# Adding the causal part of the first query tile's scores on VectorE instead of TensorE

## The reference, cut to what matters

```
x = x + moe_0(x, cond)                       # shared expert, 8 routed experts, top 2
x = x + moe_1(x, cond)
x = x + hs,  h_new = tanh(h * leak + sigmoid(h @ Wh.T + z_t @ Wz.T + b) * z_t)   # 256 steps, one after another
q, k, v = split(x @ c_attn_w + c_attn_b)     # k and v get the image token in front
scores = where(kj <= qi + 1, q . k / sqrt(8), -1e4) + mask
x = x + (softmax(scores) @ v) @ c_proj_w + c_proj_b
```

## Time and profile before

| what | value |
|---|---|
| median of 3 runs | 479.17 us (478.98 to 481.24) |
| profiled execution, time | 479.9 us |
| profiled execution, span of the instructions | 478.1 us |
| TensorE busy | 442.8 us, 93% |
| VectorE busy | 309.3 us, 65% |
| ScalarE busy | 261.2 us, 55% |
| GpSimd busy | 85.9 us, 18% |
| last step of the recurrence ends | about 343.1 us |

### The profile page before, as it was taken

How to read it: one execution, slowest core, us unless ns; L and a number is a source line. 1 busy time by engine, 2 the same in 40 slices (tenths; PEclk the granted TensorE clock), 3 DMA queues, 4 the chain that set the end, 5 groups by cost and what they waited for, 6 DMA issues and landing times.

```text
span 478.1 us, 13039 instructions
## 1 busy us (share of the span) xinstructions
PE 442.8 (93%) x4530; PEld 310.0 (65%) x4530; DVE 309.3 (65%) x999; ACT 261.2 (55%) x885; POOL 85.9 (18%) x365
## 2 busy tenths in 40 slices
PE   3999999899999999999998998999998798999984
PEld 2787787667777777776756766566655464656652
DVE  6774666666656556656557665576449978569851
ACT  3552646545646556456474356654777159764461
POOL 7120313221413213213121121211100000000000
PEclk9999999999999999999999999999999999999995
DMA  8400000000000000000000000000000001001000
GB/s 314 149 12 8 6 0 1 3 0 1 3 0 2 2 2 1 1 2 1 1 1 4 1 1 2 1 3 2 2 4 22 2 2 23 6 3 26 2 4 22
DMA packets 11222, 7.70 MB, mean 16 GB/s; under 512 B 8983, under 2 KB 10263, under 8 KB 11159
## 3 DMA queue, kind: packets, MB, share of 16 engines
q1 hardware_dynamic: 10727, 6.61, 4.5%
q10 hardware_dynamic: 432, 0.27, 0.2%
HBM read 5.39 MB, written 1.05 MB: 13 GB/s over the span
## 4 chain that ended last, share of the span: by engine, by line
PE 70%; ACT 13%; DVE 11%; issue 4%; DMA 1%; POOL 0%; ACTq 0%; DVEq 0%
PE ybk L1035 17%; PE cbk L1200 11%; PE hid L1180 7%; PE ybk L1156 6%; DVE cbk L1529 4%; ACT dd L956 4%; ACT hb L882 3%; DVE wm L1443 3%; ACT hs L961 2%; PE hid L1132 2%; PE vbk L1180 2%; PE hid L1084 2%; PE hid L1060 2%; PE hid L1053 1%; PE hid L1021 1%
## 5 line engine op out<-in xcount | busy, mean ns | idle before, releaser
L1529 DVE TENSOR_TENSOR_SCAN cbk<-dd 128x24 f32<-128x24 f32 x256 | 55.7, 218 | 102.3 <-ACT dd L956 98.9
L1200 PEld LDWEIGHTS cbk<-hs,rec 128*128 128x128 f32 x512 | 76.4, 188 | 56.2 <-ACT hs L961 49.1
L1200 PE MATMUL cbk<-hs,rec 128*128 128x8 f32 x512 | 91.5, 251 | 7.7 <-ACT hs L961 3.7
L772 POOL TENSOR_TENSOR dd<-hs,leak 128x8 f32<-128x8 f32 x256 | 55.1, 215 | 233.0 <-ACT hs L961 230.4
L1035 PE MATMUL ybk<-hg,down 128*128 128x256 f32 x352 | 95.8, 398 | 0.5 <-DVE hg L1405 0.2
L961 ACT ACTIVATE hs<-cbk 128x8 f32<-128x8 f32 x256 | 45.3, 177 | 70.5 <-DVE cbk L1529 69.2
L956 ACT ACTIVATE dd<-cbk 128x8 f32<-128x8 f32 x256 | 46.4, 181 | 61.6 <-PE cbk L1200 60.1
L1180 PE MATMUL hid<-xsp,up 128*128 128x256 f16 x528 | 73.1, 277 | 2.4 <-ACT hb L882 0.6
L1035 PEld LDWEIGHTS ybk<-hg,down 128*128 128x128 f32 x352 | 60.7, 191 | 6.3 <-DVE hg L1405 0.9
L1180 PEld LDWEIGHTS hid<-xsp,up 128*128 128x128 f16 x528 | 49.7, 105 | 10.9 <-ACT hb L882 2.9
L1156 PE MATMUL ybk<-hb,vx 128*32 128x64 f32 (+1 forms) x1536 | 38.2, 223 | 2.5 <-ACT hb L947 1.9
(11 more groups left out here) (231 smaller groups left out, 661.0 us busy)
## 6 DMA issues: line engine op xcount, KB each, us to landing
qz<-up_in SPq DMA_DIRECT2D x3, 512.0 KB, 6.8
out_dram<-silu SPq DMA_DIRECT2D x4, 256.0 KB, 2.9
x<-x_in SPq DMA_DIRECT2D x7, 128.0 KB, 8.2
down<-down_in SPq DMA_DIRECT2D x1, 768.0 KB, 8.6
att<-att_in SPq DMA_DIRECT2D x1, 743.0 KB, 9.4
down<-down_in SPq DMA_DIRECT2D x1, 640.0 KB, 6.2
kp<-mrow SPq DMA_DIRECT2D x32, 4.0 KB
qz<-rows SPq DMA_DIRECT2D x32, 2.0 KB, 1.7
```

What stands on the lines that cost most here:

```text
L772: tts(dd[:, t % ZR, 1, :, 2], hs[:, t, :], leak[:, 0:1].broadcast_to([P, B]), ALU.mult).then_inc(decay, 1)
L1200: pe.matmul(cbk[c % 2][:, o:o + B], wh, hs[:, t, :], start=False, stop=True, skip_group_check=True).then_inc(gate_pre, 1)
L1529: nc.vector.tensor_tensor_scan(vps[chunk_of(t) % 2], dd[:, t % ZR, 0].rearrange("p b o -> p (b o)"), dd[:, t % ZR, 1].rearrange("p b o -> ...
```

## The change

The list of tiles whose causal part is added by TensorE becomes empty. So the 16 units of tile 0 lose their third matmul, 16 units SC come onto VectorE, the exponentials of tile 0 read `pt` after SC, and the banks of these units are freed by VectorE. As the planner gets other units and costs, it makes all lists anew.

```
-CAUSAL_PE = (0,)
+CAUSAL_PE = ()
```

## The result

The changed kernel took 483.56 us (median of 14 runs) against 479.75 us (14 runs of the kernel before on the same chip): ratio 1.009, 95% interval 1.0065 to 1.0114. A second session gave 482.97 against 480.0 us, ratio 1.0067 (1.0037 to 1.0097). So it is 3 to 4 us slower. The forecast was 481.2 us, range 477.4 to 485.5. All ratios here leave out runs over 1.5% above the fastest of their kernel, which the medians keep, so a ratio can differ from the quotient of two medians.

What follows compares the result with a forecast made beforehand. Bounds: the recurrence to 343 us, TensorE to 360, VectorE to 380, then TensorE. Terms -1.1 - 0.4 + 2.0 + 1.5 = +2.0 us on the median of 479.17 gave a forecast of 481.2 us, range 477.4 to 485.5.

Steps and rivals of the forecast that it cites:

- The gaps of VectorE: Between scans of the recurrence: room for about six SC, so 8.8 us more VectorE work comes after 343 us.
- The list of signs: Signs for a right forecast, among them nine or ten score units behind the last step and 2 to 3 us more there.
- -0.4 us in the recurrence: Before 343 us: eleven causal matmuls removed, counting only where they push a step back; bounds 0 and -2.4 us.
- -1.1 us for the five matmuls behind the last step: In TensorE's full stretch from 343 us: five causal matmuls removed at 0.22 us each.
- The lost cover: Six units of scores and four of AV move behind the last step: +3.0 us of TensorE, counted as +2.0.
- VectorE's uncovered 1.5 us: Behind the last step: 17% of 8.8 us more VectorE work stays uncovered; bounds -1 and +8.8 us.
- The sum: Whole kernel: -1.1 - 0.4 + 2.0 + 1.5 = +2.0 us.
- the new order of the lists: All lists: reordering moves times by a microsecond or two either way, widening the range to 477.4 to 485.5 us.
- The bound of -1 us: Behind the last step: TensorE, waiting for an SC, takes up tile 2's keys sooner than 349.52 us.
- Rival A: TensorE: 3.5 us of causal matmuls leave the busiest engine, giving -1.1 - 0.4 to -3.5 us, about 477 us; chance 0.18.
- Rival B: From 343 to near 382 us: VectorE becomes the bound, +4.5 to +7.5 us, about 485 us; chance 0.20.

Runs made afterwards that it cites:

- The first eight on VectorE: The change for only the first four sequences of tile 0 (8 of 16 units), the other 8 keeping TensorE's matmul; 485.16 us, 1.0097 to the kernel before.
- the thin SC: The changed kernel in its same instruction order, but tile 0's SC works on 64 of 512 columns; 483.32 us, 1.0069 to the kernel before.
- the exchanged kernel: The change with tile 1's causal part moved to TensorE, tile 0's staying on VectorE; 486.37 us, 1.0149 to the kernel before.
- both add it: The change with TensorE's causal matmul kept for tile 0, so its causal part is added twice; 488.82 us, 1.020 to the kernel before.
- no causal part: The kernel before without tile 0's causal part on either TensorE or VectorE; 485.77 us, 1.0078 to the kernel before.
- split by place: Against the kernel before, tile 0's last two sequences go to VectorE and tile 1's last three to TensorE; 485.89 us, 1.010.
- the last pair of runs: The split of tiles 0 and 1 between TensorE and VectorE, without (485.89 us) and with twenty dummy matmuls before tile 3's bounds (478.71 us, 0.9974).

## Why the prediction was right, and where its steps were not

The direction and the mechanism were right, and the measured median lies in the range. The size was half to two thirds of what came (+2.0 against +3.8 and +3.0 us between medians), and two of its terms were mis-sized. By its steps:

- **The gaps of VectorE.** Forecast six SC before the last step; there were seven before the last scan (two of them between 302 and 306 us, where I had looked for none) and one begun just behind it. Ten units of scores and five of values were forecast before the last step and found, to the unit. (The list of signs says nine or ten units of scores *behind* the last step; that contradicts the sum, and six came there.)
- **-0.4 us in the recurrence.** Measured -0.2 at the last NEW.
- **-1.1 us for the five matmuls behind the last step.** The first eight on VectorE against the change bear it out: with six matmuls kept there, the distance grows by 1.3 to 1.5 us behind the last NEW, some 0.23 each.
- **The lost cover, +3.0, taken as +2.0.** The +3.0 was right, the 1 us taken off it was not. From the last NEW to tile 2's projection the changed kernel has 118 matmuls of scores against 106, 960 of values against 896, and no causal one against five: six units of scores and four of values more, as forecast. TensorE's busy time grew by 2.3 us (columns as in the earlier trace rows, the kernel before, then the second profile), where +3.0 - 1.1 gives +1.9:

```profile
342.93:434.07 91.14, 84.21 (x1368) 49.76 (x1367) 66.42 (x146) 58.82 (x112) 0.00 (x0) 1.00 0.04 9
342.71:437.37 94.66, 86.55 (x1446) 52.03 (x1445) 74.45 (x160) 61.88 (x117) 0.00 (x0) 1.00 0.04 8
```

  I had let 1 us of tile 1's work go into TensorE's idle time from 360 to 380 us. None did: TensorE's work from 360 to 382 us fell (17.64 to 16.99 us), and 11 instead of 6 SC of tile 1 stand behind tile 2's bounds. Each unit of tile 1 needs an SC first, and VectorE is full there. I had both rows and read them one at a time.
- **VectorE's uncovered 1.5 us.** Where I had placed it, right behind the last step, it was 0: the thin SC took away 3.9 us of VectorE there and moved no event up to tile 1's projection by over 0.05 us. But TensorE's idle time up to tile 2's projection grew by 1.2 us (6.93 to 8.11): 0.65 more from 360 to 382 us, 0.75 more from 382 to 397 us, where the 11 SC of tile 1 stand, and 0.2 less between the projections of tiles 1 and 2. The two terms together were forecast as -1.0 + 1.5 = +0.5. That this idle time hangs on tile 1's SC fits the exchanged kernel, which has none there and idles for 4.95 us; no run takes it alone.
- **The sum.** -0.2 + 2.3 + 1.2 = +3.3 us, which is what tile 2's projection shows. Tile 1's projection shows +2.0, just the forecast, but by luck: 2.1 us of other work (the values of tile 3) stand behind it in the changed kernel and ahead of it in the kernel before.
- **And the clock's chance.** Five of the first 14 runs were 4 to 9 us over the rest. No row of the kernel before could show it, and I had given the new order of the lists "a microsecond or two in either way"; seven of the twelve profiles taken after show a fall of the clock before 466 us, and it cost up to 12 us. What sets it off in one execution and not in the next stays open.
- **An error of reading.** I wrote that tile 2's keys had to wait for X3 at 343.8 us. That X3 is tile 3's; tile 2's keys need only step 192 and were held back by the order alone. The bound of -1 us that hung on it was not reached: in the change KP for tile 2 starts at 348.6, 0.9 us sooner, and it gains nothing.

Rival A (TensorE's relief decides) is out: no kernel with all of tile 0's causal matmuls taken off TensorE was faster than the one before, though the relief itself is real (5.0 us between "both add it" and the change). The rule of the Trainium skill that it leaned on, in "Perfetto Trace Analysis", section Identifying the Most-Contended Engine, does not bring the gain here that TensorE's 93% promised. The same section's warning, that matmul busy time is not a good measure of how close TensorE is to its limit, fits: TensorE's sum stayed at 442 us, while from 306 to 343 us the dummies in it grew from 8.3 to 13.5 us. Rival B (VectorE bound behind the last step) is out too: VectorE's full stretch ended at 382.2 us, as before. A part of it is true further on, in the 1.2 us of TensorE's idle time above.

## What to carry to other kernels

Work moved to an engine with 65% busy time can cost nothing where another engine is the bound, as tile 0's SC right behind the last step did, and more than it saves where it takes a gap of a chain, as in the recurrence. Count the gaps of the engine in the stretch that sets the pace, and price the *other* engine's work that then finds no place in it. A unit that passes through three engines can use one engine's idle time only if the other two have some as well. Compare two orders of work at a place where both have done the same work. And before a matmul is taken off a TensorE that is filled up with dummies, look at whether it was what held the granted clock.

## What the runs showed of the hardware

TensorE's granted clock stood at its upper level of 2.4 GHz (1.00) or at its lower of 1.2 GHz (0.50). A fall within a profile cost up to 12.4 us, more than any of the edits did at the upper level. It fell behind 4 us in which TensorE was busy 1.78 and 1.63 us of 2 (no causal part), and behind 1.43 and 0.81 of 2 (split by place); but it held in the second profile of the change behind 1.06 and 0.99 of 2 (402 to 406 us), and in the thin SC's, with the same order and the same 1.06 and 0.99, it fell. In the kernel before it held behind 1.18, 1.19 and 1.30 of 2 (398 to 404 us). So busy time alone doesn't tell, and the same lists fall in one execution and not in another. With 31 us at half clock within the recurrence the last NEW came 12.4 us late; with 20.5 us within the scores of tile 2 the lead of 2.1 us became a lag of 6.6, some 8.6 us. The Trainium skill says in "Perfetto Trace Analysis", section Matmul Optimizations, that the engine "dynamically scales power based on utilization" and that matmuls should run back to back; the last pair of runs agrees, where twenty dummy matmuls moved the median from 6.8 us above the kernel before to 1.9 below it.

The first profile of the change also shows a transfer of 2 KB, a row of tile 3 on its way into the queries, landing 3.8 us after its issue where 1.7 is the median. TensorE waited 2.2 us for it, up to 466.49 us (L1132, reading `qz`), and its clock was at half from 467.6 to 474.5 us. The profile of the kernel before has such a transfer of 3.6 us too, so the slow transfer is not of the change.
